# Second layer: a shift's low part two maxima later, and the normalised rows on GpSimd

## What is computed

```python
xn = layernorm(x)
x = x + attn(xn) + ffn(xn)

def attn(xn):                       # 16 heads of 8, chunks of 64 tokens, causal by chunk
    q, k, v = split(xn @ W_qkv.T)
    probs = softmax(q @ k.T * Dh ** -0.5)
    energy = probs.sum(-1)
    fhn = fhn_dynamics(energy)      # two explicit steps of a small recurrence
    probs = probs * (0.5 + 0.5 * sigmoid(mean(fhn)))
    return (probs / (probs.sum(-1) + 1e-8) @ v) @ W_out.T

def ffn(xn):
    r = sigmoid(mix(xn, mu_r) @ W_r.T); k = mix(xn, mu_k) @ W_k.T
    return r * (square(relu(k)) @ W_v.T)
```

## Time and profile before

| what | us |
|---|---|
| median of three runs | 1850.0 |
| profiled execution | 1852.44 |
| its span, first to last instruction | 1850.7 |
| PE busy | 1562.0 (84%) |
| VectorE busy | 1189.7 (64%) |
| ScalarE busy | 849.1 (46%) |
| GpSimd busy | 704.2 (38%) |

### The profile page before, as it was taken

How to read it: one execution, slowest core, us unless ns; L and a number is a source line. 1 busy time by engine, 2 the same in 40 slices (tenths; PEclk the granted TensorE clock), 3 DMA queues, 4 the chain that set the end, 5 groups by cost and what they waited for, 6 DMA issues and landing times.

```text
span 1850.7 us, 37612 instructions
## 1 busy us (share of the span) xinstructions
PE 1562.0 (84%) x13600; PEld 1012.6 (55%) x13600; DVE 1189.7 (64%) x2669; ACT 849.1 (46%) x1597; POOL 704.2 (38%) x1095
## 2 busy tenths in 40 slices
PE   2799999999995999999178888898888898888994
PEld 1577676777764899999033444443444443444442
DVE  2788878888874444445176676677666677667751
ACT  1344444454441334333015555655545665555662
POOL 1476675756652112122522223433423333422223
PEclk9799999999998999999558899999989998999996
DMA  3011111111102766665342344433344432343300
GB/s 94 24 45 45 41 49 36 50 34 42 47 27 54 211 208 213 212 207 173 95 90 62 55 93 92 87 66 66 61 92 93 85 71 59 64 87 75 76 8 12
DMA packets 117023, 152.72 MB, mean 83 GB/s; under 512 B 28788, under 2 KB 81652, under 8 KB 112244
## 3 DMA queue, kind: packets, MB, share of 16 engines
q1 hardware_dynamic: 103944, 120.25, 26.9%
q0 software_dynamic: 12928, 30.43, 5.9%
HBM read 109.01 MB, written 41.09 MB: 81 GB/s over the span
## 4 chain that ended last, share of the span: by engine, by line
PE 57%; DVE 27%; issue 5%; POOL 4%; DMA 2%; ACT 2%; another core or an unknown queue 1%; SPq 1%; DVEq 0%; POOLq 0%; ACTq 0%
DVE nmax L1233 9%; PE bank L1623 7%; PE bank L1614 7%; PE bank L1492 6%; PE bank L1669 6%; PE bank L1694 4%; PE bank L1544 3%; PE bank L1509 3%; PE bank L1472 3%; PE bank L1449 2%; PE bank L1644 2%; PE bank L1391 2%; PE bank L1741 2%; DVE xn L896 2%; DVE hT L1052 2%
## 5 line engine op out<-in xcount | busy, mean ns | idle before, releaser
L1233 DVE TENSOR_REDUCE nmax<-bank 128x1 f32<-128x512 f32 (+3 forms) x704 | 428.8, 632 | 211.6 <-PE bank L1669 178.6
L817 ACT ACTIVATE P<-bank 128x512 f32<-128x512 f32 x640 | 374.6, 597 | 365.8 <-PE bank L1694 292.0
L1669 PE MATMUL bank<-KT,QT 76*128 76x512 bf16 (+3 forms) x1024 | 271.9, 326 | 128.1 <-DVE nmax L1233 101.5
L1669 PEld LDWEIGHTS bank<-KT,QT 76*128 76x128 bf16 x1024 | 89.2, 101 | 332.4 <-DVE nmax L1233 244.0
L1694 PE MATMUL bank<-QT,KT 78*128 78x512 bf16 (+3 forms) x1024 | 260.5, 317 | 8.3 <-ACT P L817 5.4
L541 POOL TENSOR_TENSOR P<-P,early_w 128x512 f32<-128x512 f32 x128 | 160.7, 1280 | 144.2 <-ACT P L732 143.4
L1492 PE MATMUL bank<-P,V 128*32 128x512 f32 (+3 forms) x2048 | 205.2, 473 | 0.0
L1179 DVE TENSOR_TENSOR hT<-hr 128x512 f32<-128x512 f32 x144 | 99.5, 692 | 107.7 <-ACT hr L786 107.7
L786 ACT ACTIVATE hr<-bank 128x512 f32<-128x512 f32 x144 | 86.0, 597 | 165.8 <-PE bank L1614 165.8
L570 POOL DMA_DIRECT2D ys_d<-P x72 | 52.3, 726 | 256.1 <-DVE P L1185 241.2
L549 POOL DMA_INDIRECT xs_d<-xn,idx x128 | 137.2, 1072 | 32.5 <-issue 32.5
(11 more groups left out here) (205 smaller groups left out, 2561.4 us busy)
## 6 DMA issues: line engine op xcount, KB each, us to landing
P<-in_fc SPq DMA_DIRECT2D x72, 256.0 KB, 2.7
P<-in_proj SPq DMA_DIRECT2D x72, 256.0 KB, 2.9
QT<-parts_d SPq DMA_DIRECT2D x96, 192.0 KB
parts_d<-parts SPq DMA_DIRECT2D x32, 384.0 KB, 3.2
P<-xs_d SPq DMA_DIRECT2D x72, 128.0 KB, 2.2
ys_d<-P POOLq DMA_DIRECT2D x72, 128.0 KB, 2.8
KT<-parts_d SPq DMA_DIRECT2D x64, 128.0 KB
KT<-parts_d SPq DMA_DIRECT2D x32, 192.0 KB
```

The source lines that it names most:

```text
L817: nc.scalar.activation(P[s % 2][:, u, :], bank[k % 2][:, :], ACT.Exp, scale=float(DH) ** -0.5).then_inc(s_sb, 1)
L1233: nc.vector.tensor_reduce(nmax[:, j, h:h + nh], bank[2 + k % 2][:, 0:nh * w].rearrange("p (h w) -> p h w", h=nh), AX.X, ALU.max, negate=Tr ...
L1669: ins = pe.matmul(bank[2 + k % 2][:, i * w:(i + 1) * w], QT[n.p][0:MROWS, h, j * 128:(j + 1) * 128], KT[n.p][0:MROWS, h, 0:w], start=True, ...
```

## The change

On VectorE the low part of the second shift moves from behind the 7th to behind the 9th maximum, and most other steps of `between` slide by two maxima (the residues, low parts, the first shift's low part and reweighing too). The rows of xn are no longer made by VectorE in two pairs behind the 17th and 18th maximum; GpSimd makes them, all four, in a new function `ln_rows` that is called directly behind `ln_root` and ahead of `fhn_stimulus`. On PE `turn_xn` goes from (1, 7) to (1, 8), the `q_rows` from (2, 0) and (2, 1) to (2, 1) and (2, 2), `turn_y2` and `project_out2` one step later, and ScalarE's copies follow them.

```diff
+            def ln_rows(n):
+
+                pool.wait_ge(ln_rstd, n.at(1, 1))
+                for j in range(J):
+                    nc.gpsimd.tensor_scalar(xn[n.p][:, j, :], x1[n.p][:, j, :], mv[:, j, 0:1], rstd[:, j:j + 1],
+                                            ALU.subtract, ALU.mult).then_inc(xn_ready, 1)
...
                     ln_root(b + 2)
+                    ln_rows(b + 2)
...
-                        if at == (1, 8) and front:
+                        if at == (1, 9) and front:
                             evac_xnT(b + 2)
-                        if at == (2, 0) and before_:
+                        if at == (2, 1) and before_:
                             tanh_gate(b + -1)
-                        if at in ((2, 2), (2, 3)) and front:
-                            hi2(b + 2, u - 2)
-                        if at in ((2, 4), (2, 6)) and front:
-                            mid2(b + 2, u // 2 - 2)
+                        if at in ((2, 3), (2, 4)) and front:
+                            hi2(b + 2, u - 3)
+                        if at in ((2, 6), (2, 7)) and front:
+                            mid2(b + 2, u - 6)
...
-                        if at == (2, 7) and before_:
+                        if at == (2, 9) and before_:
                             tanh_resp(b + -1)
-                        if at == (3, 6) and before_:
+                        if at == (3, 7) and before_:
                             evac_yT(b + -1)
...
-                    if m == 7 and core:
+                    if m == 9 and core:
                         shift_low(b, 1)
-                    if m == 8 and core:
+                    if m == 10 and core:
                         gate_kv(b)
-                    if m == 9 and core:
+                    if m == 11 and core:
                         gate_residual(b)
-                    if m in (10, 12) and front:
-                        combine(b + 2, m // 2 - 5)
-                    if m == 13 and front:
+                    if m in (12, 14) and front:
+                        combine(b + 2, m // 2 - 6)
+                    if m == 15 and front:
                         ln_moments(b + 2, False)
-                    if m == 14 and before_:
+                    if m == 16 and before_:
                         y_out(b + -1, 3, (b + -1).p)
                         reweigh_den(b + -1)
-                    if m == 16 and before_:
+                    if m == 18 and before_:
                         reweigh_scale(b + -1)
-                    if m in (17, 18) and front:
-                        ln(b + 2, False, range(2 * (m - 17), 2 * (m - 17) + 2))
-                    if m in (25, 27) and front:
-                        residue2(b + 2, (m - 25) // 2)
                     if m == 24 and core:
                         y_out(b, 0, b.p)
-                    if m in (29, 31) and front:
-                        low2(b + 2, (m - 29) // 2)
-                    if m == 32 and after:
+                    if m in (27, 29) and front:
+                        residue2(b + 2, (m - 27) // 2)
+                    if m in (31, 33) and front:
+                        low2(b + 2, (m - 31) // 2)
+                    if m == 34 and after:
                         shift_low(b + 1, 0)
-                    if m == 33 and before_:
+                    if m == 35 and before_:
                         reweigh_inverse(b + -1)
-                    if m == 34 and before_:
+                    if m == 36 and before_:
                         reweigh(b + -1)
...
-                        if where == (1, 7) and front:
+                        if where == (1, 8) and front:
                             turn_xn(b + 2, False)
...
-                        if where in ((2, 0), (2, 1)) and front:
-                            q_rows(b + 2, u)
+                        if where in ((2, 1), (2, 2)) and front:
+                            q_rows(b + 2, u - 1)
...
-                        if where == (3, 4) and before_:
+                        if where == (3, 5) and before_:
                             turn_y2(b + -1)
-                        if where == (3, 8) and before_:
+                        if where == (3, 9) and before_:
                             project_out2(b + -1)
```

## The result

The changed kernel takes 1911.46 us (median of four runs, 1908.78 to 1913.51) against 1846.88 us (four runs, 1842.97 to 1854.01): ratio 1.0353, interval 1.0327 to 1.038, so 65 us slower. Its profiled execution took 1911.31 us, its span is 1909.6 us, and the mean granted clock is 0.902 (before: 0.923).

What follows compares the result with a forecast made beforehand. PE and VectorE bound the kernel in turn, losing time at the second shift's stop. Per body + 0.2 net and + 2.9 for the clock, thirteen times + 40 us on 1852.4, less 2.4: 1890 us, range 1845 to 1920.

Steps and rivals of the forecast that it cites:

- rival (a): The clock falls at both PE stops, moments come 1.8 us later in each body: 1914 us; chance 0.17.
- Part 1, the shift: Second shift's low part two maxima later: VectorE gains 1.1 us, PE's stop shrinks from 3.6 to about 1.9 us.
- Part 2: Other steps sliding by one or two maxima: same work and order, at nothing while covered; late loads at most 1.5 us.
- Part 3, the rows: Rows of xn on GpSimd: 0.58 us each, four 2.3 us, bounds 1.2 and 3.2; VectorE saves 1.0 us.
- The queue, and the wait before the reciprocal: GpSimd's rows delay the floor: VectorE waits 3.2 us between 18th and 19th maximum, in each of bodies 1 to 13.
- The sum of one body: Gains of 1.1, 1.0 and 0.9 us go into the new wait, turn of xn + 0.5: net + 0.2 us.
- The clock behind the new stop: Clock 0.50 behind PE's new stop, in the PE-bound stretch: + 2.9 us a body, as in body 7.
- Rival (b): New wait before the reciprocal comes, but no clock fall in the PE-bound part behind it: about 1852 us; chance 0.2.
- Rival (c): Rows on GpSimd near their lower bound, clock at 1.00 behind both stops: faster, 1832 us; chance 0.13.
- Rival (d): Parts' loads too late for the fifth maximum: + 1.5 us per body on top of (b), 1870 us; chance 0.05.

Runs made afterwards that it cites:

- the fillers: Changed kernel with four additional 128x512 f32 matmuls, results unused, on PE in its new stop: 1881.37 us, ratio 1.0205 against the kernel before.

## Why the prediction was right, and where its sizes were off

The forecast was 1890 us, with 1845 to 1920 as range: slower, by a new wait in front of the reciprocal and the clock behind it. The direction held, and so did the new wait and the low clock behind it. The loss was 65 us instead of 40: 1911 us lies inside the range, but outside the forecast's own 1875 to 1905, and next to the 1914 us of rival (a), the clock falling at both stops, which had a chance of 0.17. In 11 of the 13 bodies there are low stretches at both places. So the forecast was right in what happens, and too low because a term put at nothing, a mis-sized one and that rival were all on the same side.

**Part 1, the shift.** Right. The wait is gone, VectorE restarts at PE's signal, and PE's stop is 1.96 us where 1.9 were forecast. The late signals' cause, which the prediction only read off body 13, was shown by the moved gathers. But body 1, which the sum counts among the thirteen, has no late signals before, and neither has body 13; for these two the 1.1 us read from body 3 don't hold.

**Part 2, "at nothing while the cover holds".** Wrong, and this is a step that failed. The slide alone costs 15 us between the traces and 23 by the ratio. The parts' loads, the danger that the prediction named, are covered in body 3 (the last is issued by 1205.84 and PE needs it at 1211.30), but not everywhere: in after PE waits for them in bodies 1, 6 and 13, up to 2.0 us and 4.3 together. The larger thing that it missed is, as far as the traces tell, that the low stretch behind the old stop was a cheap one. The prediction itself said that its cost was hidden under VectorE; it didn't ask what follows when it is cut short.

**Part 3, the rows.** The term was mis-sized: 0.784 us each, not 0.58; four take 3.14 us. That is inside the bounds (0.29 to 0.81), at the end given by L616, not at what was made of L614. It is also just twice L614's 0.388 us for half the columns: the row may well have been the right one, and the 0.20 us taken off it as a fixed part the mistake. Even with 0.20 us taken off, an element costs (0.784 - 0.20) / 128 = 4.6 ns. The Trainium skill (GPSIMD Engine Reference, section 3.1) has 1.8 cycles an element as the best case, 1.5 ns at its 1.2 GHz (an estimate). Here the measurement decides: the operation with two operands per partition takes three times that.

**The queue, and the wait before the reciprocal.** The place is right, the number of bodies too, and the size 4.36 instead of 3.2 us; 0.8 of the 1.2 are the rows' price.

**The sum of one body, 57.9 us against 59.4 measured in body 3.** Step by step, from VectorE's restart: the moments should end after 9.5 us and end after 11.0 (1158.26 to 1169.30), with 1.36 us of waiting for PE on the way. That is rival (a)'s mechanism: the clock fell at the first stop too, PE was busy for 6.72 of the next 6.80 us at 0.50, and VectorE caught up with it. It was priced at 1.8 us and cost 1.5 here. The rival had a chance of 0.17 because the stop is half as long as before; but in the earlier trace rows the clock had fallen where PE had worked for 2.27 of 3.42 us, and here it was 1.44 of 3.40. By that row (a) deserved to be part of the forecast. From the moments to the reciprocal it is 6.9 us where 5.9 were forecast, the rows again. From the reciprocal to the next restart it is 41.5 us against 42.5 forecast (57.9 less 9.5 and 5.9). Together + 1.5 + 1.0 - 1.0 = + 1.5 us.

**The clock behind the new stop.** 0.50 is granted behind it in all thirteen bodies, and the price of 2.9 us, from body 7, fits: 2.6 us a body by the fillers. But in seven bodies the stretch had begun ahead of the stop, which the prediction doesn't have. Rival (b), the wait without the clock, is nearly what the fillers made (of the 7.1 us at 0.50 that are left, most are behind the first stop): 1881, not 1852, for it had the rows and the slide too cheap.

**Rival (c)** needed rows of 0.45 us each. **Rival (d)**, the parts' loads too late, is seen in bodies 1, 6 and 13 only.

So the 65 us are three parts of some 22 each: the slide by its own run; the rows on GpSimd at all (the slide alone against the rows behind the stimulus, 1868 to 1890 us); and their place ahead of the floor (1890 to 1911). Along the other cut, by the fillers: 31 for the clock at the new stop, and about 35 for all the rest. The parts don't simply add: the rows alone cost 93 us.

What stays open: whether the change costs as much where the signals are on time, since after wasn't run on the second chip; why the signals are late behind gathers on one chip and not on the other; and how much of the slide's 1.2 us a body is clock. No version run here beats before; the low shift moved alone and the gathers moved, on the second chip, and the small gaps filled are within 0.5% of it.

## What to carry to other kernels

An engine that is idle for 12 us of a body is still on the path in the few microseconds between one input and one output that others wait for. Work put there lengthens the path by its full duration, and that duration should be bounded by the dearest similar row, and by the nearest row scaled whole, with nothing taken off it as a fixed part. And a stop of PE has two prices, its length and the clock behind it: before a stall is moved or shortened, ask which engine is the bound in the microseconds behind the place where the low clock will be then.

## What the runs showed of the hardware that was not expected

- TensorE's clock fell to 0.50 (1.2 GHz) behind a stretch in which PE was busy for 1.44 of 3.40 us, with a stop of only 1.96 us in it, and stayed there for 6.8 us with PE busy nearly throughout.
- Filling a stop need not shorten the time at 0.50: with the old stop filled it was 7.9 us a body as in the trace of before (another chip's), stood 22 us into the body in place of 12, and the kernel was 1.3% slower than before on its chip.
- With GpSimd's indirect gathers under way PE's signals were some 3 us late on one chip (cast 4.1 us behind its transposes in place of 1.0), and on time on another, in two traces of the same kernel. The two also differ by 1.4% in the time of the kernel before.
- A matmul in f32 over 512 columns makes two records; the eight records of four took 3.70 us.
- A GpSimd operation on 128x128 with a subtraction and a multiplication by operands per partition takes 0.784 us, twice the 0.388 of L614 on 64 columns, so that the fixed part of 0.20 us read off the 128x4 operations doesn't show between these two.
